# Streaming the down weights of a scan-and-experts layer through a small ring, and giving the space to a third unit of scan output

## The reference, cut to what matters

```python
mod = (_silu(L0_c) @ L0_wmod).reshape(4, 6, 1, -1)      # sa, ca, ga, sb, cb, gb
h = _layernorm(x) * (1 + ca) + sa
u = conv_general_dilated(h, conv_w, ...) + conv_b        # 4 taps, per channel
dt, B, C = split(u @ xproj_w.T)
delta = softplus(dt @ dtproj_w.T + dtproj_b)
h_t = exp(delta * A) * h_{t-1} + delta * B * u           # for each of 16 states
y = sum over states of C * h_t, + u * D_skip
x = x + ga * y
h = _layernorm(x) * (1 + cb) + sb
scores = softmax over the top 2 of tanh(h @ Wg1.T) @ Wg2.T
x = x + gb * sum_e scores_e * (silu(h @ Wup_e.T + bup_e) @ Wdown_e.T + bdown_e)
```

## Time and profile before

| what | value |
|---|---|
| median of 3 runs | 1579.51 us (1575.52 to 1580.64) |
| profiled execution | 1578.87 us, span 1577.1 us |
| PE busy | 1391.6 us (88%) |
| VectorE busy | 1233.5 us (78%) |
| ScalarE busy | 856.5 us (54%) |
| GpSimd busy | 1109.7 us (70%) |
| moved by DMA | 97.86 MB, 62 GB/s over the span |

### The profile page before, as it was taken

One profiled execution on the slowest core, in us unless ns is written; L12 is line 12 of the kernel. 1 busy time (PEld: TensorE's weight loads), 2 busy tenths in 40 slices (PEclk: granted clock), 3 DMA queues, 4 the chain that ended last, 5 costly groups with the idle time before them and its releaser, 6 DMA issues. The chain is left out here.

```text
span 1577.1 us, 21896 instructions
## 1 busy us (share of the span) xinstructions
PE 1391.6 (88%) x7208; PEld 944.4 (60%) x7208; DVE 1233.5 (78%) x1755; ACT 856.5 (54%) x1615; POOL 1109.7 (70%) x1136
## 2 busy tenths in 40 slices
PE   7486556998999988998999988998999999998998
PEld 5273334565656666565656656566657667766665
DVE  3779999789987899789887899789987898864111
ACT  2555746474756656474656656574747554433221
POOL 0479878678886968687786978687886887753222
PEclk9656657999999999999999999999999999989999
DMA  5443111113121211212121211212121211110110
GB/s 176 149 156 133 34 53 43 44 35 94 47 67 41 73 52 39 81 36 89 49 65 41 82 43 50 71 41 94 40 75 31 67 41 64 44 35 21 24 34 25
DMA packets 64201, 97.86 MB, mean 62 GB/s; under 512 B 6988, under 2 KB 27596, under 8 KB 64088
## 3 DMA queue, kind: packets, MB, share of 16 engines
q1 hardware_dynamic: 64088, 96.47, 19.4%
HBM read 87.65 MB, written 8.79 MB: 61 GB/s over the span
## 5 line engine op out<-in xcount | busy, mean ns | idle before, releaser
L560 POOL TENSOR_TENSOR DB<-DU,BR 128x512 f32<-128x512 f32 x512 | 654.4, 1283 | 285.4 <-DVE H L860 217.9
L694 ACT ACTIVATE pb<-DELP,AN 128x512 f32<-128x512 f32 x512 | 351.8, 688 | 346.5 <-DVE H L860 344.5
L1078 PE MATMUL pb<-WD,G 128*128 128x512 f32 x1024 | 496.8, 611 | 3.0 <-POOL G L578 3.0
L1010 PE MATMUL pb<-ID,H 128*128 128x128 f32 x2048 | 340.4, 294 | 95.1 <-DVE ACC L874 67.8
L1010 PEld LDWEIGHTS pb<-ID,H 128*128 128x128 f32 x2048 | 257.8, 151 | 254.7 <-DVE ACC L874 97.1
L874 DVE SCALAR_TENSOR_TENSOR ACC<-pb,CTM,ACC 128x512 f32<-128x512 f32 x512 | 374.2, 731 | 21.7 <-PE pb L1010 20.9
L860 DVE TENSOR_TENSOR_SCAN H<-pb,ST,DB 128x512 f32<-128x512 f32 x256 | 325.6, 1272 | 16.1 <-PE pb L1010 8.5
L1059 PE MATMUL pb<-H2H,WUH 128*128 128x256 f32 x1024 | 323.9, 316 | 2.0 <-DVE TY L923 2.0
L860 DVE TENSOR_TENSOR_SCAN H<-pb,DB 128x512 f32<-128x512 f32 x256 | 309.8, 1211 | 19.2 <-ACT pb L694 11.2
L923 DVE SCALAR_TENSOR_TENSOR TY<-pb,BUP,SR 128x256 f32<-128x256 f32 x256 | 119.4, 472 | 220.5 <-ACT TY L758 220.5
L1061 PE MATMUL pb<-H2H,WUL 128*128 128x256 f32 x1024 | 291.1, 284 | 0.0
(11 more groups left out here) (125 smaller groups left out, 1167.2 us busy)
## 6 DMA issues: line engine op xcount, KB each, us to landing
BR<-bscr SPq DMA_DIRECT2D x128, 256.0 KB, 3.2
SR<-sscr SPq DMA_DIRECT2D x128, 128.0 KB, 3.2
DU<-in_x SPq DMA_DIRECT2D x8, 1024.0 KB, 7.3
ACC<-in_x SPq DMA_DIRECT2D x16, 512.0 KB, 3.8
out<-ACC SPq DMA_DIRECT2D x32, 256.0 KB, 2.9
WD<-in_wmod SPq DMA_DIRECT2D x4, 1024.0 KB, 10.4
WD<-in_wdT SPq DMA_DIRECT2D x4, 1024.0 KB, 6.9
DU<-in_xpT SPq DMA_DIRECT2D x8, 320.0 KB, 4.1
```

The source lines that it names most:

```text
L560: eng.tensor_tensor(DB[:, i % NDB], DU[:, c % 2, q], BR[:, n % 2], ALU.mult).then_inc(S["dbu"], 1)
L694: eng.activation(DA[i % NDA][:], DEL[:, c % 2, q], ACT.Exp, scale=AN[:, q, n:n + 1]).then_inc(S["da"], 1)
L1010: t = eng.transpose(b[:, dt * 128:dt * 128 + 128], src[:, dt, j * 128:j * 128 + 128], ID[:])
L1078: eng.matmul(DN[j][:], G[:, (cs * NM + m) % NG, j * 128:j * 128 + 128], WD[:, m], start=False, stop=m == NM - 1).then_inc(S[f"dn{j}"], 1)
```

## The change

The down weights are no longer kept. `WD` becomes a ring of NWD = 3 tiles that hold one pair (one expert, 512 KB) each. SP issues a load two slots before the pair starts, 128 loads in all, each of which waits for the last `dn` of the pair three before. The space goes to `H`, which holds NH = 3 units, and to a fourth `DB` tile. With this, every flip is LAG = 6 slots behind its scan's number, not 4, and a scan waits for the flips of the unit three before. The attention tasks and the even half's norm and router move two slots later, while `br`, the expert slots and the odd half's router stay. All `ys` now stand at the end of slot b + 2. The pieces of the modulation matrix are placed elsewhere (`WM[1]` in the third unit of `H`, `WM[2]` over `XH` and `TO`, `WM[3]` after `WM[0]` in the ring).

```diff
-NDA, NDB, NG = 2, 3, 3
+NDA, NDB, NG = 2, 4, 3
+NH, NWD = 3, 3
+LAG = 6
...
-TAPS = [(16, 0, 2, 1), (18, 0, 1, 1), (20, 1, 2, 1), (21, 0, 0, 0), (22, 2, 2, 1), (23, 1, 1, 0), (24, 3, 2, 1),
-        (25, 2, 1, 0), (26, 1, 0, 1), (27, 3, 1, 0), (28, 2, 0, 1), (29, 3, 0, 0)]
+TAPS = [(18, 0, 2, 1), (20, 0, 1, 1), (22, 1, 2, 1), (23, 0, 0, 0), (24, 2, 2, 1), (25, 1, 1, 0), (26, 3, 2, 1),
+        (27, 2, 1, 0), (28, 1, 0, 1), (29, 3, 1, 0), (30, 2, 0, 1), (31, 3, 0, 0)]
...
-    at += [(30, ("lddt", c)), (28, ("bcp", c)), (29, ("bcq", c, 1)), (31, ("bcq", c, 2)), (32, ("bcq", c, 3))]
+    at += [(32, ("lddt", c)), (30, ("bcp", c)), (31, ("bcq", c, 1)), (33, ("bcq", c, 2)), (34, ("bcq", c, 3))]
...
-    at += [(33, ("dtp", c)), (35, ("dtq", c, 1)), (36, ("dtq", c, 2)), (37, ("dtq", c, 3)), (38, ("dtt", c))]
+    at += [(35, ("dtp", c)), (37, ("dtq", c, 1)), (38, ("dtq", c, 2)), (39, ("dtq", c, 3)), (40, ("dtt", c))]
     for dt in range(4):
-        s = 42 + 2 * dt
+        s = 44 + 2 * dt
...
-    at += [(51, ("ln", c))]
+    at += [(53, ("ln", c))]
     for dt in range(4):
-        s = 52 + 2 * dt
+        s = 54 + 2 * dt
         at += [(s, ("del", c, dt)), (s + 1, ("du", c, dt)), (s + 2, ("ud", c, dt))]
...
-        stats, norm, turn, route = 2, 5, 7, 11
+        stats, norm, turn, route = 4, 7, 9, 13
...
-    at = [(b + o, 0, ("up", cs, m)), (b + 2, 0, ("th", cs, m)), (b + 2, 1 - o, ("ys", cs, m)),
+    at = [(b + o, 0, ("up", cs, m)), (b + 2, 0, ("th", cs, m)), (b + 2, 0, ("ys", cs, m)),
...
         at.append((b - 2, 0, ("sr", cs, m // 2)))
+        at.append((b - 2, 0, ("wd", cs, m // 2)))
...
-    at = [(b + o, 0, ("up", cs, m)), (b + 2, 0, ("th", cs, m)), (b + 2 + o, o, ("ys", cs, m)),
+    at = [(b + o, 0, ("up", cs, m)), (b + 2, 0, ("th", cs, m)), (b + 2, 0, ("ys", cs, m)),
...
-    for g in range(4):
-        place(13 + 3 * g, 0, ("wd", g))
...
-        turns.setdefault(i + 4, []).append(("flip", c, n, j))
+        turns.setdefault(i + LAG, []).append(("flip", c, n, j))
     for c in range(NC):
-        for s, j in ((0, 2), (2, 3), (5, 0), (7, 1)) if c else ((2, 2), (3, 3), (5, 0), (7, 1)):
+        for s, j in ((0, 2), (3, 3), (7, 0), (9, 1)) if c else ((3, 2), (4, 3), (7, 0), (9, 1)):
...
-        WM = [WDv[:, 0], WDv[:, 1], WDv[:, 2], WDv[:, 3], DEL[:, 1], DU[:, 1]]
+        WD0 = WD[:, 0:2].rearrange("p r k d -> p (r k) d")
+        WM = [WD0, H[:, 2], XT[:].rearrange("p (k d) -> p k d", k=4), WD0, DEL[:, 1], DU[:, 1]]
...
-                    g = k[0]
-                    eng.wait_ge(S["modp"], nth["rows", g])
-                    eng.dma_start(WDv[:, g], wd_v[g]).then_inc(S[f"d_wd{g}"], 16)
+                    cs, e = k
+                    i = cs * NE + e
+                    if i >= NWD:
+                        eng.wait_ge(S["dn1"], 2 * (i - NWD) + 2)
+                    elif i == 0:
+                        eng.wait_ge(S["modp"], nth["rows", 3])
+                    eng.dma_start(WD[:, i % NWD], wd_v[e]).then_inc(S[f"d_wd{i % NWD}"], 16)
...
-                    if q == 0 and c * NS + n >= 2:
-                        pc, pn = divmod(c * NS + n - 2, NS)
+                    if q == 0 and c * NS + n >= NH:
+                        pc, pn = divmod(c * NS + n - NH, NS)
                         eng.wait_ge(S["flip"], nth["flip", pc, pn, 3])
...
-                        if cs == 0 and m % 4 == 0:
-                            eng.wait_ge(S[f"d_wd{m // 4}"], 16)
+                        if m % 2 == 0:
+                            eng.wait_ge(S[f"d_wd{(cs * NE + m // 2) % NWD}"], 16 * ((cs * NE + m // 2) // NWD + 1))
```

More of the change, by code:

```diff
@@ L34, in attention_slots @@
     for dt in range(4):
-        s = 13 + 2 * dt
+        s = 15 + 2 * dt
         at += [(s, ("tr", c, dt)), (s + 1, ("hm", c, dt)), (s + 2, ("u3", c, dt))]
-    at += [(21, ("hc", c)), (21, ("ldxp", c))]
+    at += [(23, ("hc", c)), (23, ("ldxp", c))]
     for s, dt, tap, one in TAPS:
         at += [(s, ("conv", c, dt, tap))] if one else [(s - 1, ("cvs", c, dt, tap)), (s, ("cva", c, dt, tap))]
-    at += [(30, ("lddt", c)), (28, ("bcp", c)), (29, ("bcq", c, 1)), (31, ("bcq", c, 2)), (32, ("bcq", c, 3))]
@@ L41, in attention_slots @@
-    at += [(33, ("bct", c)), (34, ("bw", c)), (34, ("ct", c)), (35, ("ctm", c))]
-    at += [(33, ("dtp", c)), (35, ("dtq", c, 1)), (36, ("dtq", c, 2)), (37, ("dtq", c, 3)), (38, ("dtt", c))]
+    at += [(32, ("lddt", c)), (30, ("bcp", c)), (31, ("bcq", c, 1)), (33, ("bcq", c, 2)), (34, ("bcq", c, 3))]
+    at += [(35, ("bct", c)), (36, ("bw", c)), (36, ("ct", c)), (37, ("ctm", c))]
+    at += [(35, ("dtp", c)), (37, ("dtq", c, 1)), (38, ("dtq", c, 2)), (39, ("dtq", c, 3)), (40, ("dtt", c))]
     for dt in range(4):
-        s = 42 + 2 * dt
-        at += [(39 + dt, ("ug", c, dt)), (s, ("dz", c, dt)), (s + 1, ("ab", c, dt)), (s + 1, ("m", c, dt)),
+        s = 44 + 2 * dt
+        at += [(41 + dt, ("ug", c, dt)), (s, ("dz", c, dt)), (s + 1, ("ab", c, dt)), (s + 1, ("m", c, dt)),
@@ L211, in adaln_kernel @@
         DB = sb("DB", [128, NDB, CT])
-        H = sb("H", [128, 2, 4, CT])
+        H = sb("H", [128, NH, 4, CT])
         G = sb("G", [128, NG, FT])
         TY = sb("TY", [128, 4 * FT])
-        XH = sb("XH", [128, 4 * FT])
-        TO = sb("TO", [128, 2, D])
+        XT = sb("XT", [128, 4 * D])
+        XH = XT[:, 0:4 * FT]
+        TO = XT[:, 4 * FT:4 * D].rearrange("p (j d) -> p j d", j=2)
         TH = TY[:, 0:2 * FT].rearrange("p (s t) -> p s t", s=2)
@@ L223, in adaln_kernel @@
         WUL = sb("WUL", [128, 4, 2048], f32r)
-        WD = sb("WD", [128, NM, D])
+        WD = sb("WD", [128, NWD, 2, D])
         GB = sb("GB", [128, D])
@@ L252, in adaln_kernel @@
         STT = sb("STT", [NE, FT])
-        XN2 = XH[:].rearrange("p (j d) -> p j d", j=2)
-        H2F = XH[:].rearrange("p (j d t) -> p d j t", j=2, d=4)
+        XN2 = XH.rearrange("p (j d) -> p j d", j=2)
+        H2F = XH.rearrange("p (j d t) -> p d j t", j=2, d=4)
         HHV, HLV = [[z[:, h].rearrange("p d (j t) -> p d j t", j=2) for h in range(2)] for z in (H2H, H2L)]
-        WS = [XH[:], TY[:]]
+        WS = [XH, TY[:]]
         banks = [ctx.enter_context(nc.psum_tensor(f"pb{i}", [128, 512], f32)) for i in range(8)]
@@ L266, in adaln_kernel @@
         wu_v = wupT.rearrange("(k p) (h n) -> k h p n", p=128, h=2)
-        wd_v = wdT.rearrange("(g k p) o -> g p k o", p=128, k=4)
+        wd_v = wdT.rearrange("(e k p) o -> e p k o", p=128, k=2)
         CTX = H[:, 1, 3, 0:16].rearrange("p (k b) -> p k b", k=4)
@@ L270, in adaln_kernel @@
         MT1, MT2 = H[:, 1, 3, 32:48], H[:, 1, 3, 48:64]
-        WDv = WD[:].rearrange("p (g k) d -> p g k d", g=4)
-        WM = [WDv[:, 0], WDv[:, 1], WDv[:, 2], WDv[:, 3], DEL[:, 1], DU[:, 1]]
+        WD0 = WD[:, 0:2].rearrange("p r k d -> p (r k) d")
+        WM = [WD0, H[:, 2], XT[:].rearrange("p (k d) -> p k d", k=4), WD0, DEL[:, 1], DU[:, 1]]
         GR0, GR1 = ACC[0:4, 8], ACC[0:4, 9]
@@ L305, in adaln_kernel @@
                      "d_wg2", "d_bup", "d_bdn", "d_xa0", "d_xa1", "d_xp", "d_dtp", "d_bw", "d_br0", "d_br1", "d_gs",
-                     "d_gb", "d_wu0", "d_wu1", "d_wd0", "d_wd1", "d_wd2", "d_wd3", "d_sw", "d_sr0", "d_sr1", "d_o0",
+                     "d_gb", "d_wu0", "d_wu1", "d_wd0", "d_wd1", "d_wd2", "d_sw", "d_sr0", "d_sr1", "d_o0",
                      "d_o1", "d_o2", "d_o3"):
@@ L373, in _ @@
                     eng.dma_start(WM[4], wm_v[4]).then_inc(S["d_wm4"], 16)
+                    eng.wait_ge(S["modp"], nth["rows", 0])
                     eng.dma_start(WM[3], wm_v[3]).then_inc(S["d_wm3"], 16)
@@ L431, in _ @@
                         eng.wait_ge(S["wlo"], 2 * (i - 1))
+                    elif i == 0:
+                        eng.wait_ge(S["modp"], nth["rows", 2])
                     eng.dma_start(WS[h], wu_v[kk, h]).then_inc(S[f"d_wu{h}"], 16)
                 elif what == "wd":
-                    g = k[0]
-                    eng.wait_ge(S["modp"], nth["rows", g])
-                    eng.dma_start(WDv[:, g], wd_v[g]).then_inc(S[f"d_wd{g}"], 16)
+                    cs, e = k
+                    i = cs * NE + e
+                    if i >= NWD:
+                        eng.wait_ge(S["dn1"], 2 * (i - NWD) + 2)
+                    elif i == 0:
+                        eng.wait_ge(S["modp"], nth["rows", 3])
+                    eng.dma_start(WD[:, i % NWD], wd_v[e]).then_inc(S[f"d_wd{i % NWD}"], 16)
                 elif what == "sw":
@@ L700, in _ @@
                     eng.wait_ge(S["scan"], slot(c, n, 3) + 1)
-                    eng.activation(ST[:, n], H[:, n % 2, :, CT - 1], ACT.Copy).then_inc(S["st"], 1)
+                    eng.activation(ST[:, n], H[:, (c * NS + n) % NH, :, CT - 1], ACT.Copy).then_inc(S["st"], 1)
                 elif what == "whi":
@@ L850, in _ @@
                     i = slot(c, n, q)
[L851 to L854, removed]
-                    if q == 0 and c * NS + n >= 2:
-                        pc, pn = divmod(c * NS + n - 2, NS)
```

(17 more changed lines are left out.)

4 lines of the change are left out of this document (2 added, 2 removed).

## The result

| | before | changed |
|---|---|---|
| median | 1580.08 us (4 runs, 1575.52 to 1580.66) | 1599.2 us (4 runs, 1592.86 to 1600.62) |
| ratio | | 1.012, 95% interval 1.0086 to 1.0153 |
| span of the profiled execution | 1577.1 us | 1598.1 us |
| granted clock of TensorE, mean | 0.929 | 0.915 |

A forecast was written before the change was run, and what follows sets the result against it. No engine was full; loss lay between them, with PE and VectorE nearly matched and slots 28 to 47 PE's. Terms summed to -22.8 us from 1578.9, plus 0.6 for the median: 1557 us, range 1530 to 1592.

The forecast's parts named there:

- the sentence on the projections: PE's stretch, slots 28 to 47: projections move from 28 to 37 to 30 to 39, stay inside, at no cost.
- the border of the chunk: Rival, chance 0.15: at slot 64 PE stops at the flip of U behind a late GpSimd; slower, 1592 us.
- the ring: Down weight loads: term of nothing, hidden by margins; as rival, chance 0.05, SP or `br` is late, 1600 us and more.
- Flips two slots later and three units: Slots 48 to 63: PE's scan waits end; half of at most 4.2 us per chunk comes back, -12.6 us.
- the rival that wins them all: Chance 0.17: the loops come apart fully and all 40.3 us of PE's scan waits come back; 1529 us.
- another wait takes over: Rival, chance 0.13: banks keep PE and VectorE within about two slots, waits are only renamed; 1579 us.
- The fourth DB tile: GpSimd may run one slot further ahead, set against one more `du` close in front of `fin`: 0.
- One tap leaves VectorE's stretch: Slots 0 to 27: one 1.3 us tap moves into PE's stretch, where VectorE has idle time; -7.8 us.
- One dz leaves PE's stretch: Slots 28 to 47: one `dz` step of 0.86 us passes into slots 48 to 63; -5.2 us.
- All ys after acc: Where the fast experts change halves, `to` no longer stands behind an early `ys`; -4 us once, between 0 and -6.
- Tail: Last flips, even router and norm come two slots later, `r1` directly after its evacuation; +2 us, between 0 and +4.
- Ports: Rival, chance 0.05: a denser GpSimd slows VectorE's taps to their maximum and the gain is gone; 1580 us.

The follow-up runs named there:

- e1_fill: Changed kernel with the four transposes of the flip in slot 30 (chunks 1 to 6) written eight times: 1565.97 us, ratio 0.9916.
- e6_lag4: e2_proj_old with flips 4 slots behind again and the flips of U at their old slots: 1563.58 us, ratio 0.9904.
- e12_two_units: e6_lag4 with H used as two units and the later fin and out of e8_fin_late: 1561.73 us, ratio 0.9899.
- e7_ndb3: e2_proj_old with three DB tiles instead of four: 1579.68 us, ratio 0.9993.
- e2_proj_old: Changed kernel with only the projections back at their slots of before, two slots earlier: 1567.43 us, ratio 0.9912.
- e4_buffers: Kernel before with the ring of down weights, three units of H and four DB tiles, the rest as before: 1590.97 us, ratio 1.0068.
- e11_buf_fill: e4_buffers with the transposes of the flip in slot 29 (chunks 1 to 6) written three times: 1581.67 us, ratio 1.0007.
- e3_ring: Kernel before with the ring of down weights alone; slots, lag, two units and three DB tiles as before: 1578.93 us, ratio 0.9993.
- e10_ys_old: e2_proj_old with both ys at their places of before: 1570.8 us, ratio 0.9949.
- e8_fin_late: e2_proj_old with fin and out of the last half of chunk 6 seven slots later, behind the tail's router: 1566.31 us, ratio 0.9919.

## Why the prediction was wrong

**The step that failed** is the sentence on the projections: "The projections move too (28 to 37 becomes 30 to 39) but stay inside; their cover is the same." I cost the move at nothing because the work stays in PE's stretch. I did not ask which bank `bcp` takes in its new slot, who empties it, and what that engine does first. Before, in slot 28, it took the bank that `acc` empties at the end of VectorE's slot 27, and waited 0.47 us. Now, in slot 30, it takes the one that `acc` empties in VectorE's slot 29, behind the tap and `to` of slot 28. What that wait of 3.5 us set off, the fall of the clock in front of PE's own stretch, costs 33 us (e1_fill: 1599.2 to 1566.0). I had the row for it: "PE waits 2.93 us for it and then runs its next matmuls at the lower clock". I used it for one term of -4 and not as a price for any new wait. No rival named it; the slower rivals (the border of the chunk, the ring) did not happen.

Without the fall, the kernel is at 1566 to 1567 us, where I had 1557. The terms:

- *Flips two slots later and three units* (-12.6): nothing. With the lag of 4 the waits for scans are some 52 us in the steady part and the time is the same or lower (e6_lag4), and two units do as well as three (e12_two_units). The waits were also misread: I added 30.1 us at the weight load and 10.2 at the matmul, but all 17 of the second kind lie inside the first, so there were 30.1 us to win at most, not 40.3, and the rival that wins them all would be at 1539, not 1529. The wait is slack that is passed from one name to another. That was my rival "another wait takes over", to which I gave 0.13.
- *The fourth DB tile* (0): some 12 us by the medians (e7_ndb3 against e2_proj_old), as much as the whole gain. I set it against the extra `du` in front of `fin`. In the traces the tile is worth 3.1 us in the last stretch of a chunk, and without it slots 56 to 63 go from 19.5 to 22.4 us (20.6 before). With all else as before it did not pay (e4_buffers, and e11_buf_fill with the clock kept up).
- *One tap leaves VectorE's stretch* (-1.3 a chunk): slots 0 to 27 of chunk 3 go from 79.4 to 76.1 or 76.7 us. In part this is chance in the earlier trace rows: e3_ring has the same slots and its chunk 3 is 2.3 us shorter. Over chunks 2 to 6 slots 0 to 27 take 77.7 us in the mean before and 77.6 in e3_ring, 75.5 in the changed kernel and 76.3 in e2_proj_old. That is 1.3 to 2.2 us less a chunk, the forecast size or more, but the norms and flips moved in this stretch too, and no experiment moved the tap alone.
- *One dz leaves PE's stretch* (-0.9 a chunk): the stretch did not get shorter. It is 57.1 us in e2_proj_old and 57.7 in e1_fill, against 56.6 before and the 55.7 of the forecast. No experiment moved `dz` alone, so where the 1.4 us of e2_proj_old come from stays open. The 0.6 on top in e1_fill may be the moved projections.
- *All ys after acc* (-4 once): right in place and wait, and near in size: 2.9 us become 0.6, chunk 7 is 6.7 us longer without it, and the median 3.4 (e10_ys_old). Of the 1 us by which each of chunks 2 to 6 is shorter there, 0.3 lies in slots 48 to 63, the same in every chunk, and is a cost that I did not foresee; most of the rest lies in slots 0 to 27, which differ as much between other runs.
- *Tail* (+2): +4.1 us, just past the end of its range (0 to 4). PE's wait for the router's selection, with `fin` in its way on GpSimd, grew from 3.7 to 5.0 us and is 3.5 in e8_fin_late, where the tail is 3.3 us shorter. I had looked at PE's order only. Where the rest of the 4.1 us comes from stays open.
- *The ring* (0): right (e3_ring). `br` lands in 3.3 us (3.2 before), a down load in 4.8.
- *Ports* (rival): taps last 1.26 us in the median in the changed kernel, not longer. It did not happen.

`ln` and the router at slot 13 (+2.4 each) were not tested apart.

## What to carry to other kernels

When a task that takes a rotating buffer is moved, work out which buffer it gets in the new place, which instruction empties it, and what stands before that instruction on its engine. On TensorE price a wait not at its length but at its length and the half-speed matmuls behind it, and look whether they lie where TensorE sets the pace; filling the wait with harmless repeated transposes is a cheap test of it. A table of waits shows where slack sits, not what it is worth: here 52 us of one kind came back and the time did not get longer. And add up the waits of one engine only once: a wait seen at the weight load and at the matmul behind it is one wait.

## What the runs showed of the hardware

The clock does not need a long single wait to fall. It fell behind a wait of 3.49 us (to 0.50, for about 14 us in chunk 3 and about 10 in chunks 2, 4 and 6) and behind 2.2 us left of one (0.88 over the 15 us of the four slots). In e4_buffers it fell in three chunks and stayed up in two, with waits of 0.71 to 0.73 us in all of them; 0.9 us of extra transposes kept it up in all five. In the kernel before, on the other hand, PE waits 1.09 us in front of the flip of slot 35 of chunk 3, and the clock stays at 1.00:

```profile
649.71 0.66 PE L1010 MATMUL pb<-ID,H 128*128 128x128 f32 x4 [1.09 <-DVE ACC L874]
```

So what decides must be more than the length of one wait, and which chunk is hit can change with small shifts: in e6_lag4 the clock fell for 3.4 us between slots 31 and 32 of chunks 4, 5 and 6, with no wait of PE above 0.5 us in slots 26 to 35, and slots 32 to 35 took 13.6 to 13.7 us there and 12.0 to 12.1 in chunks 2 and 3.
